# The two graph layers' loops of 48 edge tiles written out with constant numbers on TensorE, VectorE and ScalarE

## The reference, cut to what matters

```
N = 12501 nodes, DIM = 128, B = 512 sessions of L = 50 items, LAYERS = 2, 150000 edges
h = emb; acc = emb
for _ in range(LAYERS):
    h = segment_sum(adj_val[:, None] * h[adj_col], adj_row, num_segments=N)
    acc = acc + h
graph_item_embs = acc / 3
combined = graph_item_embs[items] + item_features[items]
... attention over the 50 rows of each session -> select [512, 128]
scores = select @ l2norm(graph_item_embs).T          # [512, 12501]
```

## Time and profile before

| | us |
|---|---|
| median of 3 runs | 4880.22 (4876.70 to 4895.26) |
| the profiled execution | 4876.94 |
| its span, first to last instruction | 4875.2 |
| sort stage, to the first gather of layer 0 | 770.4 |
| layers, first gather to last | 3646 |
| rest (features, sessions, scores) | 458 |

### The profile page before, as it was taken

One profiled execution on the slowest core, in us unless ns is written; L12 is line 12 of the kernel. 1 busy time (PEld: TensorE's weight loads), 2 busy tenths in 40 slices (PEclk: granted clock), 3 DMA queues, 4 the chain that ended last, 5 costly groups with the idle time before them and its releaser, 6 DMA issues.

```text
span 4875.2 us, 49210 instructions
## 1 busy us (share of the span) xinstructions
PE 2918.3 (60%) x9798; PEld 1762.3 (36%) x9798; DVE 3020.2 (62%) x7277; ACT 871.3 (18%) x3002; POOL 2982.7 (61%) x3071
## 2 busy tenths in 40 slices
PE   4988884555555555555555555555555555554688
PEld 2777772223232232232232232233323323322344
DVE  8999994556555555565554555555555555555455
ACT  1898990000000000000000000000000000004443
POOL 1566666666666666666664666666666666664660
PEclk7888886677767677777667777777777776776789
DMA  0000001111111111111114111111111111133273
GB/s 31 3 3 3 3 3 43 46 45 46 46 45 45 43 46 46 45 46 46 45 44 139 45 46 45 45 46 46 45 45 46 46 46 45 45 98 86 43 116 140
DMA packets 140400, 235.54 MB, mean 48 GB/s; under 512 B 56692, under 2 KB 84272, under 8 KB 140144
## 3 DMA queue, kind: packets, MB, share of 16 engines
q0 software_dynamic: 96288, 178.10, 15.7%
q1 hardware_dynamic: 41476, 55.61, 3.4%
q10 hardware_dynamic: 2508, 0.60, 0.1%
HBM read 193.16 MB, written 41.01 MB: 48 GB/s over the span
## 4 chain that ended last, share of the span: by engine, by line
PE 14%; issue 11%; DVE 11%; another core or an unknown queue 9%; DVEq 4%; ACT 1%; DMA 0%; POOL 0%; SPq 0%; ACTq 0%
PE bank L1330 9%; DVE acc L1063 6%; DVE ring L1018 3%; PE bank L1406 2%; DVEq L1063 1%; DVEq L1059 1%; PE bank L1434 1%; DVEq L1060 1%; PE bank L1393 1%; DVEq L1053 1%; DVEq L1083 1%; PE bank L1368 1%; PE bank L1375 0%; ACT big L666 0%
## 5 line engine op out<-in xcount | busy, mean ns | idle before, releaser
L1330 PE MATMUL bank<-ring 128*128 128x256 f32 x4992 | 1969.4, 520 | 1654.7 <-DVE ring L1018 1053.4
L1330 PEld LDWEIGHTS bank<-ring 128*128 128x128 f32 x4992 | 1060.0, 244 | 2543.8 <-DVE ring L1018 1482.4
L1063 DVE TENSOR_TENSOR acc<-acc,bank 128x256 f32 x2496 | 1028.0, 412 | 1373.8 <-remote 634.8
L507 POOL DMA_INDIRECT ring<-table,cring x1248 | 1180.3, 946 | 661.6 <-issue 351.6
L507 POOL DMA_INDIRECT ring<-in_L_rec_emb,cring x1248 | 1180.9, 946 | 628.3 <-issue 356.7
L1018 DVE TENSOR_SCALAR ring<-bank,mlo,mval 128x256 f32<-128x256 f32 x2496 | 1341.3, 537 | 22.0 <-DMA ring<-table,cring 11.0
L592 ACT COPY mlo<-ring 128x24 f32 (+1 forms) x104 | 22.0, 211 | 3394.9 <-PE bank L1330 2703.9
L576 ACT ACTIVATE big<-big 128x68 f32<-128x68 bf16 x1764 | 558.8, 406 | 3.2 <-issue 3.2
L1272 PE MATMUL bank<-big,ring 128*128 128x136 f32 x2352 | 439.5, 331 | 90.1 <-issue 26.7
L479 POOL DMA_INDIRECT sorted_edges<-moved,block_to x313 | 392.0, 1252 | 101.4 <-issue 101.3
L1272 PEld LDWEIGHTS bank<-big,ring 128*128 128x128 f32 x2352 | 362.4, 222 | 165.3 <-ACT big L576 107.6
(11 more groups left out here) (202 smaller groups left out, 1641.8 us busy)
## 6 DMA issues: line engine op xcount, KB each, us to landing
scores<-stage SPq DMA_DIRECT2D x48, 512.0 KB
ring<-in_L_rec_emb,cring POOLq DMA_INDIRECT x1248
ring<-table,cring POOLq DMA_INDIRECT x1248
table<-big SPq DMA_DIRECT2D x7, 896.0 KB, 7.9
combined<-ring SPq DMA_DIRECT2D x7, 896.0 KB, 8.2
sorted_edges<-moved,block_to POOLq DMA_INDIRECT x313
ring<-combined,sidi POOLq DMA_INDIRECT x200
sorted_edges<-acc SPq DMA_DIRECT2D x1, 1248.0 KB, 4.4
```

The costliest lines, as they stand in the source:

```text
L507: pool.indirect_dma_start(msg[:, s, :], None, source, bass.IndirectOffsetOnAxis(cring[:, s:s + 1], 0)).then_inc(s_g[s], 16)
L1063: dve.tensor_tensor(acc[:, bass.ds(off, BUCKET)], acc[:, bass.ds(off, BUCKET)], bank[u % PR][:, 0:BUCKET], ALU.add).then_inc(s_acc, 1)
L1330: pe.matmul(bank[u % PR][:, 0:BUCKET], msg[:, h * T + u, :], onehot[:, u % SR, :], start=True, stop=True).then_inc(s_mm, 1)
```

## The change

The three engines' loops over rounds are replaced by plain Python loops, so that each round is emitted with constant numbers. Nothing is computed in another order, and no wait is dropped or added: each compares with a constant now instead of with a register.

```diff
@@ ScalarE
-            with act.Fori(1, NST // 2) as i:
-                for h in range(2):
-                    fetch(0, 2 * i + h, h)
+            for c in range(2, NST):
+                fetch(0, c, c % 2)
...
-            with act.Fori(0, LOOP // 2) as i:
-                for h in range(2):
-                    emb_rows(2 * i + h, h)
-                    fetch(1, 2 * i + h + 2, h)
-            for c in range(LOOP, max(NB, NST - 2)):
+            for c in range(max(NB, NST - 2)):
@@ VectorE
-                with dve.Fori(0, LOOP // 2) as i:
-                    for h in range(2):
-                        round_step(layer, 2 * i + h, i, h)
-                for c in range(LOOP, NST):
+                for c in range(NST):
                     round_step(layer, c, c // 2, c % 2, last=(c == NST - 1))
@@ TensorE
-                for c in range(2):
-                    products(layer, c, c)
-                    if layer == 1:
-                        transpose_embeddings(c, c)
-                with pe.Fori(1, LOOP // 2) as i:
-                    for h in range(2):
-                        products(layer, 2 * i + h, h)
-                        if layer == 1:
-                            transpose_embeddings(2 * i + h, h)
-                for c in range(LOOP, NST):
+                for c in range(NST):
                     products(layer, c, c % 2)
                     if layer == 1 and c < NB:
                         transpose_embeddings(c, c % 2)
```

## The result

The changed kernel takes 5006.2 us, the median of 4 runs (4996.2 to 5016.6), and the kernel before 4882.8 us, the median of 4 on the same chip. The ratio is 1.025, with a 95% interval of 1.022 to 1.029. The forecast was 4893 us with a range to 4985, so the time lies outside it. The profiled execution took 5016.6 us, its span is 5014.9.

A forecast was written before the change was run, and what follows sets the result against it. The prediction took the layers to be bound by cycles of GpSimd gathering between gates while VectorE's instruction stream slows. An occasional long cycle added 12 us to 4876.94, giving 4889 profiled and a median of 4893, range 4825 to 4985.

The forecast's parts named there:

- The mechanism: Layers: fewer VectorE and TensorE instructions delay the slow stretch, so GpSimd sometimes gathers 24 tiles, not 16, between stops.
- long cycle: Layers: 24 gathers between two GpSimd stops in 36.6 us, 2.4 us over short ones of 16 in 22.8 us.
- Fast stretches: VectorE in the layers: additions 0.78 us apart, up to 16 instead of 13 or 14, before its instruction stream slows.
- the second gate: GpSimd's wait 16 gathers, 20 us, after a start; if passed, eight more tiles follow and the stop is 7 us.
- signs of being wrong: Layers: other cycle lengths, fast stretches still ending after 13 additions, a vanished gap, or changes the cycles don't account for.
- the choice between the mixtures: Loop rounds: three or six short cycles to one long, +27 or -3 us; the middle, +12, was taken.
- the second rival: Layers: mostly long cycles, since a start on tile 8 repeats itself; 4969 to 5061 us, chance 22%.
- whole mixed case: Layers: short cycles with a long one now and then, -3 to +50 us, chance 45%.
- The session work: Ends of rounds: session work or embedding block, some ten instructions, shortens the fast stretch by one addition.
- Long cycles take over: Layers: the second gate is passed at most starts; 4969 us at the proportion seen, 5061 with long ones alone, chance 22%.
- The turns: Loop branches on VectorE and TensorE: removal costed at nothing, between -34 and 0 us; as a stall of their own, 4%.
- the fetches: Written-out code: about 120 more instruction fetches, costed at nothing, or +30 us if each of VectorE's held it; chance 2%.

The follow-up runs named there:

- e10c: The changed kernel with GpSimd's gates at every sixth tile (PACE 6 in place of 8), on a chip with slow stretches: 4836.3 us, ratio 0.988.
- b0_before: The kernel before, unchanged, run again with a trace on a chip without slow stretches: median 4315 us.
- e3: The kernel before with VectorE's loops alone written out: 4912.3 us, ratio 0.991.
- e4: The kernel before with TensorE's loops alone written out: 4932.6 us, ratio 0.993.
- e7c: The changed kernel with one semaphore increment more per addition and per product, on a chip with slow stretches: 4920.0 us, ratio 1.005.
- p1b: The changed kernel with three stretches of 300 VectorE writes before the layers, on a chip with slow stretches: the one beside gathers took 34.7 us.
- p1: The changed kernel with three stretches of 300 VectorE writes before the layers, on a chip without slow stretches: 9.2 to 9.5 us each.
- e1: The changed kernel with one already met wait more per tile in front of VectorE's additions: 5017.1 us, ratio 1.013 to the kernel before.

## Why the prediction was wrong

- **The mechanism was right for layer 0 of this chip, and in part for layer 1.** Cycles were to be 22.8 or 36.6 us long; they are 23.0 and 36.8. A long cycle was to cost 2.4 us over short ones; it costs 36.75 - 1.5 x 22.98 = 2.3. Fast stretches were to hold up to 16 additions, the second gate to be passed 20 us after the start, the stop to grow from 3 to 7 us. Each is in the rows above. The prediction had no place for the pairs of 16 and 8, and in layer 1 most starts on tile 0 are followed by 12 or 13 fast additions, which is one of its own signs of being wrong. e10c shows that the second gate is what lets a cycle become long: with gates at 6, 12 and 18 none does.
- **The step that failed** is the choice between the mixtures: "I choose between the last two. A short cycle moves the start by 16 within the round of 24, so starts fall on tiles 8, 0 and 16 in turn. In rows 2 the starts on tile 16 (2459.1 and 4302.7) gave short cycles, and only starts on tile 8 gave long ones". It made a rule of six cycles, none of which started on tile 0. It also went against the prediction's own remark under the second rival, that a start on tile 8 repeats itself after a long cycle: if every visit of tile 8 gave a long cycle, the chain would never leave tile 8 and there could be no three short ones to one long. In the changed kernel the starts on tile 0 are the long ones (48 of the 57 single ones; 3 start on tile 8 and 6 on tile 16), and since a long cycle moves by a whole round, the next start is on tile 0 again. In layer 0 the chain locks; in layer 1 it doesn't. The share was to be one long cycle in four to seven, 20 to 33% of the gathers, and is 82%. In time the step was sized at +12 us (-3 to +50 for the whole mixed case) and measured +129 in the layers.
- **The session work does not protect.** The work at each round's end was to shorten the fast stretch by an addition in either layer. The cycle of layer 0 shown has it inside its fast stretch (L1034 at 1216.98), and still has 16 fast additions. In layer 1 the embedding block goes with a stretch that is shorter by three or four, and that layer lost 34.6 us of the 129. That the block is what does it is argued: no run takes it out.
- **The rival was priced right and held too unlikely.** "Long cycles take over" said that a start repeats itself after a long cycle, 4969 us at the proportion seen and 5061 with long ones alone; 5006 lies between. It had 22%, on the evidence that three of six written-out cycles were long. Those six were the only full cycles in the changed form, and taken at their word, without a rule on tiles, they gave 4969. Two slips of a point or two decide nothing: the sum gives 4892 where 4893 stands, and the cases as weighed add up to 31% faster, 30% within and 39% slower.
- **The turns** were costed at nothing, between -34 and 0, and **the fetches** at nothing or +30. On the chips without slow stretches the loops and the written-out code are within 0.001 of each other, so both are worth about 5 us at most there, where GpSimd's pace would hide a loss of VectorE's. On the first chip the layers' extra 129 us are told by the mixture (133 worked out), and the cycles themselves are hardly longer, 36.8 us for 36.6 and 23.0 for 23.1. That leaves at most some 10 us for fetches, not 30.
- **The register instructions** are gone and some 110 fetches are there, as said (180 and 57 on the two queues over the whole span, 105 and 23 before).
- **What was not seen at all** is that the slow stretches belong to some of the chips. The trace had a sign of it: the earlier trace rows name "remote" as the releaser of waits for `s_mm` or `s_acc`, which TensorE's products and VectorE's additions raise, so semaphore events of the core's own engines are missing; the page of b0_before names "remote" nowhere. And no gather has a time to landing.

What stays open: why some chips have slow stretches, whether the same chip always has them, and whether they are there when nothing records the events. Every run here was taken with the span and clock of its core, so none shows the kernel without a record. That the chips with slow stretches lose 70% of the semaphore events points to the recording, and is argued, not shown. Open too is what decides between short and long beside the count of instructions. With nine instructions a tile the share is 12% (e3) and 28% (e4), with ten 5% (before, in loops) and 30% (e7c, written out), so the count alone doesn't order the kernels.

## What to carry to other kernels

When the time of a loop is made of cycles between two gates, a faster part can move the system from one number of tiles per cycle to the next, and the next may be worse; look at how near the slowest engine is to the second gate when it is reached, and how a cycle moves the next start. A pattern that reproduces its own starting point can take over, as it did in layer 0, so its share in a few cycles is no estimate of its share in the end. Before a difference of 2% is taken for the kernel's, run both kernels on more than one chip: here it was 1.025 on one and 1.000 on three.

## What the runs showed of the hardware

- While GpSimd issues gathers by index, on some chips VectorE starts instructions singly or in groups of up to 12, 0.70 or 1.40 us apart, after a first fast part, and goes on so for 3.7 us after the last gather (p1b). Direct moves by SyncE, 24 of 64 KB, have no such effect within 9.5 us, though they move 132 GB/s in place of 52.
- In that slow stretch the trace holds 103 semaphore events of the landings of 24 gathers, and for SyncE's 24 moves 384 (p1b; 384 and 384 on the other kind of chip, p1).
- On the other chips the same 300 instructions take 9.2 us, and the kernel 4314 us in place of 4883: the kind of chip is worth 12%, more than the change.
- A wait that is added in front of an instruction can cost no instruction: two semaphore waits ride on one (e1, 52 recorded instructions more for 2496 waits).
- More instructions can make a kernel faster: 2496 semaphore increments on each of two engines took the changed kernel's layers from 3732 to 3646 us on one chip, and from 78% of its gathers in rounds of 24 to 30% (p1b, e7c).
